# A conditional MLP: shorter warm-up, a first weight chunk rounded in halves, a second one loaded in halves, and the EPS addition of one tile pair on GpSimd

## The reference

```
0 (NR):  out = gelu(x @ w1_nr + b1_nr) @ w2_nr + b2_nr              512x512, 512x512
1 (TSR): out = gelu(x @ w1_tsr + b1_tsr) @ w2_tsr + b2_tsr          the same shapes
2 (SR):  h = gelu(x @ w1_sr + b1_sr)                                512x1024
         out = gelu(h @ w2_sr + b2_sr) @ w3_sr + b3_sr              1024x512, 512x512
y = x + out
result = (y - mean(y)) * rsqrt(var(y) + EPS) * gamma + beta         over the 512 features
```

## Time and profile before

| | us |
|---|---|
| Median of 3 runs | 559.62 (559.47 to 559.8) |
| The profiled execution's own time | 559.41 |
| Its span, first to last instruction | 557.7 |
| PE busy in the span | 549.6 |
| DVE, ACT, POOL busy | 273.9, 213.5, 248.3 |

### The profile page before, as it was taken

One profiled execution on the slowest core, in us unless ns is written; L12 is line 12 of the kernel. 1 busy time (PEld: TensorE's weight loads), 2 busy tenths in 40 slices (PEclk: granted clock), 3 DMA queues, 4 the chain that ended last, 5 costly groups with the idle time before them and its releaser, 6 DMA issues. The chain is left out here.

```text
span 557.7 us, 8222 instructions
## 1 busy us (share of the span) xinstructions
PE 549.6 (99%) x2423; PEld 453.4 (81%) x2424; DVE 273.9 (49%) x448; ACT 213.5 (38%) x328; POOL 248.3 (45%) x196
## 2 busy tenths in 40 slices
PE   9999999999999999999999999999999999999994
PEld 6888888888888888888888888888888888888883
DVE  5660176775856956114710569112765105601657
ACT  5451336145244354214421452424255124513351
POOL 0979898765674575300430046600174300430056
PEclk9999999999999999999999999999999999999998
DMA  8876405245344444200320044400244100410032
GB/s 313 339 237 190 152 7 196 100 151 188 109 155 145 156 150 141 84 0 0 138 87 0 1 158 142 150 0 0 75 150 159 66 0 29 154 43 0 0 135 91
DMA packets 26370, 61.28 MB, mean 110 GB/s; under 512 B 3058, under 2 KB 3314, under 8 KB 26226
## 3 DMA queue, kind: packets, MB, share of 16 engines
q1 hardware_dynamic: 26208, 60.97, 31.9%
q10 hardware_dynamic: 146, 0.13, 0.1%
HBM read 44.31 MB, written 16.78 MB: 110 GB/s over the span
## 5 line engine op out<-in xcount | busy, mean ns | idle before, releaser
L467 DVE TENSOR_TENSOR g_lo<-bank,g_hi 128x512 fp32r<-128x512 f32 x112 | 77.5, 692 | 251.0 <-DVEq L117 250.9
L415 ACT ACTIVATE g_hi<-bank,bcol 128x512 fp32r<-128x512 f32 x112 | 77.9, 695 | 165.9 <-ACTq L117 164.7
L620 POOL TENSOR_TENSOR rstd<-var_eps,power 128x2 f32<-128x2 f32 x30 | 21.0, 699 | 239.7 <-POOLq L117 239.7
L616 POOL TENSOR_TENSOR y<-y,row 128x512 f32<-128x512 f32 x64 | 95.7, 1514 | 49.1 <-POOLq L117 48.9
L437 ACT ACTIVATE y<-y,rstd 128x512 f32<-128x512 f32 x63 | 42.3, 717 | 166.3 <-ACTq L117 166.3
L244 PE MATMUL bank<-w_hi,g_hi 128*128 128x512 f32 x256 | 99.6, 389 | 0.0
L245 PE MATMUL bank<-w_lo,g_hi 128*128 128x512 f32 x256 | 99.6, 389 | 0.0
L246 PE MATMUL bank<-w_hi,g_lo 128*128 128x512 f32 x256 | 99.6, 389 | 0.0
L244 PE MATMUL bank<-x_hi,w_hi 128*128 128x512 f32 x240 | 93.4, 389 | 0.0
L245 PE MATMUL bank<-x_lo,w_hi 128*128 128x512 f32 x240 | 93.4, 389 | 0.0
L246 PE MATMUL bank<-x_hi,w_lo 128*128 128x512 f32 x240 | 93.4, 389 | 0.0
(11 more groups left out here) (42 smaller groups left out, 580.2 us busy)
## 6 DMA issues: line engine op xcount, KB each, us to landing
y<-x SPq DMA_DIRECT2D x64, 256.0 KB, 3.6
out<-y SPq DMA_DIRECT2D x63, 256.0 KB, 2.5
stage<-x_t SPq DMA_DIRECT2D x31, 512.0 KB, 3.3
w_raw<-weights SPq DMA_DIRECT2D x17, 512.0 KB, 5.1
row<-rows SPq DMA_DIRECT2D x1, 1280.0 KB, 11.0
stage<-x_t SPq DMA_DIRECT2D x2, 256.0 KB, 3.2
w_raw<-weights SPq DMA_DIRECT2D x2, 256.0 KB, 4.0
out<-y SPq DMA_DIRECT2D x1, 128.0 KB, 1.9
```

The costliest lines, as they stand in the source:

```text
L415: eng.activation(g_hi[:, slot, :], psum, ACT.Gelu, bias=b)
L467: eng.tensor_tensor(g_lo[:, slot, :], psum, g_hi32[:, slot, :], ALU.subtract).then_inc(s_gs, 1)
L616: eng.tensor_tensor(y[:, t, :], y[:, t, :], row[:, kind, :], ALU.add).then_inc(s_xb, 1)
L620: eng.tensor_tensor(rstd[:, t:t + n], var_eps[:, t:t + n], power[:, t:t + n], ALU.pow).then_inc(s_rstd, n)
```

## The change

The warm-up is 15 matmuls of 307 columns and 7 of 128, where it was 9 of 512 and 14 of 128. The second weight chunk of layer 1 is loaded in two DMAs of 256 columns (128 KB) each, with a semaphore for each. DVE rounds each of the first two weight chunks in two halves of 256 columns, and PE waits for a half before the first of the two blocks j that lie in it. In every batch but the last, the EPS addition for tiles 0 and 1 moves from DVE to POOL, where it runs just ahead of the power; a semaphore `s_moments` hands the variance over, and POOL waits for its own addition by `s_eps`. Tiles 2 and 3 and the last batch keep DVE's addition.

```diff
--- before.py
+++ after.py
@@ -38,7 +38,7 @@
 FINISHED_BY_OTHERS_END = TT - 1
 
 
-N_WARM, N_WARM_SHORT = 9, 14
+N_WARM, N_WARM_SHORT, WARM = 15, 7, 307
 
 
 def conditional_mlp(nc, x, x_t, cond, weights, bias_cols, rows, out):
@@ -87,7 +87,7 @@
 
 
         s_x_piece = [sem(f"s_x_piece{c}") for c in range(2)]
-        s_w_piece = [sem(f"s_w_piece{c}") for c in range(2)]
+        s_w_piece = {(c, n): sem(f"s_w_piece{c}_{n}") for c, n in ((0, 0), (1, 0), (1, T // 2))}
         s_loaded = {(g, n): sem(f"s_loaded_{g}_{n}") for g, (_, count) in PAIRS.items()
                     for n in range(1 if g == "nr" else 0, count)}
         s_full = [sem(f"s_full{f}") for f in range(2)]
@@ -104,7 +104,7 @@
         s_y, s_acc = sem("s_y"), sem("s_acc")
         s_row = [sem(f"s_x_row{t}") for t in range(TT)]
         s_xb, s_ev, s_bn, s_mv = sem("s_xb"), sem("s_ev"), sem("s_bn"), sem("s_mv")
-        s_var = sem("s_var")
+        s_moments, s_eps, s_var = sem("s_moments"), sem("s_eps"), sem("s_var")
         s_own = sem("s_own")
         s_rstd, s_rstd_end = sem("s_rstd"), sem("s_rstd_end")
         s_v, s_v_end = sem("s_v"), sem("s_v_end")
@@ -192,7 +192,9 @@
             for c in range(2):
                 n = slice(c * T, c * T + T)
                 eng.dma_start(stage[:, 0, c, :], x_halves[0][:, n]).then_inc(s_x_piece[c], 16)
-                eng.dma_start(w_raw[:, c, :], weights[0][:, n]).then_inc(s_w_piece[c], 16)
+
+                for h in ((slice(0, T),) if c == 0 else (slice(0, T // 2), slice(T // 2, T))):
+                    eng.dma_start(w_raw[:, c, h], weights[0][:, c * T + h.start:c * T + h.stop]).then_inc(s_w_piece[c, h.start], 16)
             load_x(x_halves[1], 1)
             load_pair(("nr", 1))
             eng.dma_start(bcol[:, :], bias_cols).then_inc(s_const, 16)
@@ -287,7 +289,6 @@
                     take(eng, s_x01, 1)
                     for c in range(2):
                         eng.wait_ge(s_first, c + 1)
-                        eng.wait_ge(s_first_w, c + 1)
                         for which in range(3):
                             if which == 1:
                                 if c == 0:
@@ -298,6 +299,8 @@
                             if which == 2:
                                 eng.wait_ge(s_nr, 2 + c)
                             for j in range(HC):
+                                if which == 0 and j % 2 == 0:
+                                    eng.wait_ge(s_first_w, 2 * c + j // 2 + 1)
                                 part(j, c, which)
                         if c == 0:
                             read_next()
@@ -370,7 +373,7 @@
                 last_layer(W3[SR], ORDER_SR, claim=False)
 
             for _ in range(N_WARM):
-                eng.matmul(bank[7][:, :], ones[:, 0:P], ones, start=True, stop=True)
+                eng.matmul(bank[7][:, 0:WARM], ones[:, 0:P], ones[:, 0:WARM], start=True, stop=True)
             for _ in range(N_WARM_SHORT):
                 eng.matmul(bank[7][:, 0:P], ones[:, 0:P], ones[:, 0:P], start=True, stop=True)
             eng.sem_inc(s_acc, 4)
@@ -525,7 +528,11 @@
                     stats(kind, t + 1)
                     moments(kind, t)
                     moments(kind, t + 1)
-                    variance(t, 2)
+                    if t == 0:
+                        take(eng, s_mv, 2)
+                        eng.sem_inc(s_moments, 2)
+                    else:
+                        variance(t, 2)
                     centre(kind, t)
                     centre(kind, t + 1)
 
@@ -566,10 +573,12 @@
                 lo(w_lo[:, c, :], w_raw[:, c, :], w_hi32[:, c, :], n_first, s_nr)
 
             for c in range(2):
-                eng.wait_ge(s_w_piece[c], 16)
-                eng.tensor_copy(w_hi[:, c, :], w_raw[:, c, :]).then_inc(s_first_w, 1)
+                for half in (slice(0, H // 2), slice(H // 2, H)):
+                    if (c, half.start) in s_w_piece:
+                        eng.wait_ge(s_w_piece[c, half.start], 16)
+                    eng.tensor_copy(w_hi[:, c, half], w_raw[:, c, half]).then_inc(s_first_w, 1)
                 x_low(c, c + 1, (s_nr, s_x01)[c])
-                eng.wait_ge(s_first_w, c + 1)
+                eng.wait_ge(s_first_w, 2 * c + 2)
                 w_low(c, 0)
             x_low(2, 3, s_nr)
             x_low(3, 4, s_x23)
@@ -616,7 +625,13 @@
                         eng.tensor_tensor(y[:, t, :], y[:, t, :], row[:, kind, :], ALU.add).then_inc(s_xb, 1)
 
             def deviations(t, n):
-                take(eng, s_var, n)
+
+                if t == 0:
+                    take(eng, s_moments, n)
+                    eng.tensor_scalar(var_eps[:, t:t + n], mv[:, t:t + n, 1], EPS, None, ALU.add).then_inc(s_eps, n)
+                    take(eng, s_eps, n)
+                else:
+                    take(eng, s_var, n)
                 eng.tensor_tensor(rstd[:, t:t + n], var_eps[:, t:t + n], power[:, t:t + n], ALU.pow).then_inc(s_rstd, n)
 
             def deviation_end(t, done=s_rstd):
```

## The result

The changed kernel takes 560.85 us (median of 13 runs, 560.47 to 561.1), the kernel before 559.62 (13 runs beside them, 559.43 to 560.43). The ratio is 1.0019, 95% interval 1.0011 to 1.0027. The forecast was 559.2, with a range from 558.6 to 559.8. The direction was wrong and the range missed by 1.05 us. The profiled execution of the changed kernel took 560.59 us, with a span of 558.6.

A forecast was written before the change was run, and what follows sets the result against it. PE, busy without a gap from 6.00 to 550.40 us, was taken to bound the kernel. The terms -0.40 + 0 + 0 + 0 = -0.40 took the median from 559.62 to 559.2 us, range 558.6 to 559.8.

The forecast's parts named there:

- What bounds the kernel: Whole span: PE busy 544.40 of 544.40 us; a change helps by starting PE earlier without opening a hole.
- the sum's "+ 0 + 0 + 0": Total over the edits: rounding in halves, the split load and EPS on POOL each put at 0 us.
- The shorter warm-up: PE's start: first real load from 6.00 to 5.25 us, clock rise unmoved, so 0.40 us gained.
- The term of 0.40: PE's start: 899 real columns done earlier at the slow clock, worth 0.40 us.
- Rounding in halves: Weight chunk 0 on DVE: two halves take 0.56 us, later DVE work 0.13 late, cost to PE nothing.
- The second chunk in two loads: Layer 1 loads: everything behind 0.3 us later, covered by margins; cost nothing, at worst about 0.6 us.
- EPS on POOL: Tiles 0 and 1, 15 batches: 0.8 us more on POOL, DVE up to 1.1 earlier in batch 0; cost nothing.
- the 32.5 named: Sign to look for in batch 0: DVE's second variance comes before 32.5 us.
- the place nearest to PE: Batch 1: POOL's remainder ending at 43.60, needed by the matmul of 44.32, a margin of 0.7 us.
- The first: Rival at PE's start: clock rises with the warm-up's end, full 0.75 us won, 558.87 us; chance 0.18.
- The second one: Rival: PE waits at chunk 1, chunk 2 or batch 1's split, price 0.4 to 0.6, 559.6 to 559.8; chance 0.17.
- The slower rival: Rival at the start: clock rises later, each us costing half a us, up to 561.9; chance 0.07.

The follow-up runs named there:

- e9: Changed kernel with SP holding back the POOL_ALL weight loads until POOL's first bias addition in batch 0; 559.39 us, ratio 0.9993.
- e10: Kernel before without the branch prefetch hints in PE's four bodies; 562.37 us, ratio 1.0046.
- e8: Changed kernel with the warm-up of before (9 x 512, 14 x 128), other edits kept; 561.15 us, ratio 1.0027.
- e4: Changed kernel with 8 short warm-ups of 112 columns for 7 of 128; 560.94 us, ratio 1.0019.
- e11: Kernel before with the first two weight chunks rounded in halves and PE waiting on halves; 560.80 us, ratio 1.0013.
- e15: Kernel before with the EPS split, POOL_ALL loads held back and a warm-up of 9 x 512 and 7 x 128; 559.02 us, ratio 0.9990.
- e16: Kernel before with the EPS split, POOL_ALL loads held back and the warm-up of before; 559.19 us, ratio 0.9993.
- e5: Kernel before with a warm-up of 9 x 512 and 7 x 128 columns; 559.64 us, ratio 0.9997.
- e6: Kernel before with a warm-up of 9 x 512 and 14 x 64 columns; 559.76 us, ratio 1.0002.
- e13: Kernel before with DVE rounding the first two weight chunks in halves, PE waiting once per chunk; 559.80 us, ratio 1.0006.
- e2: Kernel before with the second weight chunk in two loads, nothing else; 559.82 us, ratio 1.0001.
- e1: Changed kernel with the second weight chunk in one load again; 560.66 us, ratio 1.0019.
- e3: Kernel before with the new warm-up (15 x 307, 7 x 128) alone; 560.46 us, ratio 1.0008.
- e14: Kernel before with PE's waits on halves alone, DVE rounding whole chunks; 559.87 us, ratio 1.0004.
- e12: Kernel before with the EPS addition of tiles 0 and 1 on POOL alone; 559.31 us, ratio 0.9989.
- e7: Kernel before with a warm-up of 15 x 307 and 14 x 128 columns; 560.41 us, ratio 1.0015.

## Why the prediction was wrong

**What bounds the kernel** was right as far as it went: PE without a gap, and everything decided by when it begins and whether a hole opens. That PE never waits is shown for the one profiled execution alone. The step that failed is the sum's "+ 0 + 0 + 0": nothing was put down for a hole behind the start. I looked for holes where PE waits for data, with margins for each, and took PE's own instructions as always there. The profile of before showed q8 instruction packets, and I did not ask what they were or what their margin was (2.2 us at the first jump to the SR body). The missing term is +1.43 us; e9 removes it with all other edits kept, and without the hints (e10) a hole of 2.6 us stands at the same place.

**The shorter warm-up.** The start moved to 5.26 as computed. That the clock would rise at the same moment was wrong for the single execution: it gave 0.63 us, because the rise came 0.5 us earlier. It isn't tied to the warm-up's length either: in e8, with the warm-up of before, the first real matmul is at 5.07 where before it was at 6.07 (the clock rose while the last long warm-up ran, between 3.8 and 4.1 us), and in e4, with the short one, loads stay at 0.33 us until 6.36 and are fast from 6.78. By the clock events of the traces the rise lies at 3.5 us in e11, 3.9 in e8, 5.7 in the changed kernel, 6.2 before and 6.8 in e4. The moment wanders over some 3.3 us between executions, and rows 3 were one draw. The page "TensorE: Matmul & The Clock Gate" of the Trainium skill says in its section "What's actually happening" that the moment varies from run to run, by 0.5 us to either side; the traces agree that it varies, but by far more, and the traces decide. I set the variation aside because three times lay within 0.33 us. The landing of the first loads wanders too: the first weight chunk was there at 4.43 or at 6.34, the second at 7.05 or at 8.47, and with the later ones the data decide when PE begins and not the warm-up. Over the later runs the kernel before spreads from 558.80 to 561.0. The term of 0.40 measures as 0.17 between the medians of e15 and e16, which the intervals don't tell from nothing; by itself, in e5 and e6, it is nothing.

**Rounding in halves.** Cost 0.06 us on DVE against 0.13 forecast. By itself it brings no hole (e13), but with PE's waits it brings the late block (e11), which I had priced at nothing.

**The second chunk in two loads.** Forecast 0.3 us of delay, seen 0.5 to 0.6 in the changed profile, and no effect on the time that can be measured (e2). Even the 0.5 can't be laid to it: the first SR weights reach POOL at 13.6 in before and in e1, at 14.2 in the changed kernel and at 14.4 in e2, but also at 14.5 in e3, whose loads are those of before.

**EPS on POOL.** The mechanism was right, its size on POOL too dear (0.22 us for 0.6), and its worth underrated (DVE's second variance came at 32.59 for 32.97, just short of the 32.5 named): I took POOL's split of rows 7, with 0.7 us, as the place nearest to PE. Nearer is the chain to batch 1's first remainder, with 0.5 us, and it is used up where data land later: e2, e5, e6 and e14, whose end of batch 0 is that of before, wait 0.1 to 0.7 us for it at 38 to 40 us. So the EPS split is worth 0.4 us in the median (e12; its interval of 0.9980 to 0.9999 only just leaves out 1) and not nothing.

**Rivals.** The first named the full 0.75 us; the 0.63 at the start came near it, but by an early rise of the clock in this execution. The second one had the right shape, a gain given back at a later wait, but the wrong place, and its price of 0.4 to 0.6 us was about a third of the 1.43. The places that it names do cost in other profiles: at chunk 1 PE waits 0.3 us in e3 and 0.5 in e6, at chunk 2 0.7 in e8 and e9. The slower rival (a late clock) didn't happen in the changed kernel.

Open is why the first block is late in some kernels and not in others. It goes with the new long warm-ups and with the halves on both engines, by the times it differs between runs of one program (e3), and neither two instructions more or fewer (e4, e5, e6, e7) nor PE's early arrival at the jump (e2) decides it. In before and in e2, e6, e12, e13 and e14, whose loads aren't held back, the block comes at 21.2 to 22.3 while data transfers are at their fullest. So the queue isn't closed to it. Whether it gets in may hang on when it is asked for; no view shows that moment, and no run tests it.

## What to carry to other kernels

When PE has no gap, its program is a resource as well: list the instruction packets of the trace, and treat each first jump to a large body as a wait with a margin of its own, above all while bulk loads are queued. Holding such loads back until they are needed cost nothing that could be measured here and took the hole away. And a margin or a clock read from one execution is one draw: before spending 0.4 us of it, look how far the runs of the kernel spread.

## Not expected of the hardware

- A block of 16 KB of instructions, transferred in about 1.0 us, started at 21.3 us before and at 24.3 after the change, with data loads queued both times. PE could begin the new part of its program 4.4 to 4.5 us after the start of the block, in eight kernels, and stood up to 1.6 us for it; without the prefetch hint 2.6 us.
- TensorE's clock rose to its fast level at 3.5 us in one execution (e11) and at 6.8 in another (e4), with PE at work from 0.8 us on in both.
- A first load of 256 KB of weights, issued at 1.22 us as the second load in both, was usable at 4.4 us in one execution (before) and at 6.3 in another (e13).
- An addition on 128x2 takes GpSimd 0.22 us, a power on the same shape 0.72.
